# Two-block attention and expert kernel on one core: the context's five products in fp16 parts, correlation factors read from PSUM, and a new order of the step

## What is computed

```python
x = x + L0_xattn(layernorm(x), ctx, ctx)   # autocorrelation: keys and values are both ctx
x = x + L0_ffn(layernorm(x))               # base weight 1024x1024 + 8 experts of rank 16, top 2
x = x + L1_xattn(layernorm(x), ctx)        # 8 heads, window of 16, channels are the 128 rows
x = x + L1_ffn(layernorm(x))               # 4 experts of rank 16, top 2
# L0_xattn: corr = ifft(fft(q) * conj(fft(k))); top 9 lags, softmax of them;
#           out = sum_i w_i * v[min(lag_i + pos, 127)]
# L1_xattn: k = Wk ctx + bk, v = Wv ctx + bv, q = Wq x + bq, softmax over 16 neighbours, Wo
```

## Time and profile before

| what | value |
|---|---|
| median of 3 runs | 2022.52 us (2021.28 to 2024.9) |
| the profiled execution | 2025.97 us |
| its span, first to last instruction | 2024.1 us |
| mean granted TensorE clock | 0.969 |
| busy: PE, DVE, ACT, POOL | 92%, 75%, 67%, 54% |
| weight loads (PEld) | 56% |
| DMA | 45 GB/s mean |

### The profile page before, as it was taken

How to read it: one execution, slowest core, us unless ns; L and a number is a source line. 1 busy time by engine, 2 the same in 40 slices (tenths; PEclk the granted TensorE clock), 3 DMA queues, 4 the chain that set the end, 5 groups by cost and what they waited for, 6 DMA issues and landing times. The chain is left out here.

```text
span 2024.1 us, 49212 instructions
## 1 busy us (share of the span) xinstructions
PE 1855.6 (92%) x18912; PEld 1131.0 (56%) x18912; DVE 1519.6 (75%) x4529; ACT 1347.2 (67%) x1958; POOL 1088.4 (54%) x902
## 2 busy tenths in 40 slices
PE   4889999999999999999999999999999999999975
PEld 2355555665555655555565655566555565655543
DVE  6677777778777778777877777777777877877743
ACT  4267776677776677776667777667777666777652
POOL 2565555466555466555556655546655645655541
PEclk8899999999999999999999999999999999999985
DMA  5001110011111011111001111001111110111000
GB/s 217 22 33 53 52 52 31 31 52 41 52 52 36 27 50 41 52 52 52 31 31 43 50 52 52 31 31 49 45 52 52 44 39 31 41 52 42 21 6 17
DMA packets 25165, 91.56 MB, mean 45 GB/s; under 512 B 3184, under 2 KB 3312, under 8 KB 24624
## 3 DMA queue, kind: packets, MB, share of 16 engines
q1 hardware_dynamic: 25136, 91.17, 12.8%
HBM read 74.39 MB, written 16.78 MB: 45 GB/s over the span
## 5 line engine op out<-in xcount | busy, mean ns | idle before, releaser
L548 PE MATMUL pb<-w_base_h,even_words 128*128 128x512 f16 x1024 | 324.8, 379 | 0.4 <-ACT mid_t L851 0.4
L1370 POOL TENSOR_TENSOR p_hl<-sc,p_hl 128x512 f16<-128x512 f32 x128 | 178.1, 1391 | 180.3 <-ACT p_hl L730 180.3
L450 PE MATMUL pa<-ctx_a,tab 128*128 128x512 f32 x384 | 203.4, 655 | 35.6 <-ACT q_spec L730 24.3
L840 ACT ACTIVATE q_diag<-sc,par 32x1024 f32<-32x1024 f32 x192 | 216.1, 1141 | 19.9 <-DVE sc L1100 17.5
L1413 POOL TENSOR_TENSOR sc<-sc,sc_rec 128x512 f32<-128x512 f32 x128 | 134.2, 1048 | 146.8 <-DVE sc_rec L1176 146.8
L548 PE MATMUL pb<-w_base_l,even_words 128*128 128x512 f16 x512 | 193.9, 379 | 0.0
L617 PEld LDWEIGHTS pc<-sc_t,v_diag 128*128 128x128 f16 x6144 | 173.8, 97 | 32.9 <-issue 23.8
L450 PE MATMUL pa<-xn_a,tab 128*128 128x512 f32 x384 | 186.3, 609 | 1.5 <-ACT xn_a L730 1.5
L617 PE MATMUL pc<-sc_t,v_diag 128*128 128x32 f16 x6144 | 173.9, 177 | 6.5 <-ACT rows_c L730 6.5
L594 PE MATMUL pc<-k_h,q_diag 128*128 128x32 f16 x2048 | 169.1, 177 | 0.0
L595 PE MATMUL pc<-k_l,q_diag 128*128 128x32 f16 x2048 | 168.5, 177 | 0.0
(11 more groups left out here) (149 smaller groups left out, 5068.5 us busy)
## 6 DMA issues: line engine op xcount, KB each, us to landing
x_a<-in_x SPq DMA_DIRECT2D x32, 512.0 KB, 3.3
ctx_a<-in_ctx_in SPq DMA_DIRECT2D x32, 512.0 KB, 3.2
x_res<-in_x SPq DMA_DIRECT2D x32, 512.0 KB, 3.9
ctx_b<-in_ctx_in SPq DMA_DIRECT2D x32, 512.0 KB, 4.0
out<-rows_c SPq DMA_DIRECT2D x32, 512.0 KB, 2.9
v_diag<-in_base_w SPq DMA_DIRECT2D x4, 1024.0 KB, 10.1
tab<-in_spectra SPq DMA_DIRECT2D x1, 576.0 KB, 5.2
q_diag<-in_ra SPq DMA_DIRECT2D x1, 544.0 KB, 13.8
```

The source lines that it names most:

```text
L450: last = mm(place[:, n + h, :], lhsT, moving[:, h * HALF:(h + 1) * HALF], start=True, stop=True)
L548: mm(pb[:, h, :], rows[:, cols], weights[:, j, h * HALF:(h + 1) * HALF], start=(j == 0 and m == 0), stop=False)
L840: nc.scalar.activation(q_diag[rows, :, col:col + QB], source, ACT.Copy, scale=par[rows, a:a + 1]).then_inc(qd_out.sem, 1)
L1370: g_.tensor_tensor(part[:, :, :, LO], sc[:, g % 2, :, :], part[:, :, :, HI], ALU.subtract)\
```

## The change

1. **The context's products.** The context is loaded once a batch (`ctx_f`). ACT copies it to fp16 (`ctx_high`), POOL subtracts (`ctx_low`), into one of two slots of `ctx_hl`. The five tables or weights that meet it (`w_ctx_h`, `w_ctx_l`) are split once. `project_ctx` takes three fp16 matmuls for each half where `project` took a float32 one, for `a_context`, both `a_context_long`, `b_keys` and `b_values`.
2. **Experts.** `b_base_end` becomes six fp16 matmuls, `c_delta` four (high and low halves of the activations are stacked over 128 partitions), `c_mid` one fp16 transposition instead of two float32, `b_mid` two fp16 for one float32. `gates` ends with two more DVE instructions that split `mid`, once for each expert layer. `c_result` is done in two halves.
3. **Correlation's factors.** `q_spec` and the copy to it are gone. DVE forms both products, straight from PSUM. `a_values` is three copies (two of 64 partitions, one of 128) instead of four of 64.
4. **Keys and values** are computed in `pa`, in mid-step, between pieces of the base layer.
5. **Order.** The step is cut at another place (it begins with `a_context_long`), spans indices i to i-3, and is written out for two steps at a time, since the slot alternates. On every engine the calls stand in a new order. `a_corr` is halved, with a long product between the halves.
6. **Start.** All fp16 splits of weights on DVE now stand in one place, after the softmax of batch 0; ACT's stand after the exponents of batch 0. The first `a_context` waits for the split of `ctx_w` and of the context.

```diff
+            def project_ctx(n, slot, table):
+                high, low = ctx_hl[:, slot, 0, :], ctx_hl[:, slot, 1, :]
+                for h in range(2):
+                    cols = slice(h * HALF, (h + 1) * HALF)
+                    mm(pa[:, n + h, :], w_ctx_h[:, table, :], high[:, cols], start=True, stop=False)
+                    mm(pa[:, n + h, :], w_ctx_h[:, table, :], low[:, cols], start=False, stop=False)
+                    last = mm(pa[:, n + h, :], w_ctx_l[:, table, :], high[:, cols], start=False, stop=True)
+                return last
...
+            def ctx_high(b, slot):
+                act.wait_ge(ctx_read.sem, ctx_read.after(b))
+                if not early(b):
+                    act.wait_ge(mm_k.sem, mm_k.after(b - 2))
+                    act.wait_ge(mm_v.sem, mm_v.after(b - 2))
+                copy(ctx_hl[:, slot, 0, :], ctx_f[:, :]).then_inc(ctxh_out.sem, 1)
...
             def a_product(b):
-                dve.wait_ge(q_out.sem, q_out.after(b))
+                dve.wait_ge(mm_q.sem, mm_q.after(b))
                 dve.wait_ge(v_out.sem, v_out.after(b, 2))
-                v.tensor_tensor(c1[:, :], q_spec[:, :], v_re[:, :], ALU.mult).then_inc(prod_q.sem, 1)
+                if not first(b):
+                    dve.wait_ge(mm_agg.sem, mm_agg.after(b - 1))
+                v.tensor_tensor(c2, pa_hi, v_im[:, :], ALU.mult).then_inc(prod_q2.sem, 1)
+                dve.wait_ge(v_out.sem, v_out.after(b))
+                v.tensor_tensor(c1[:, :], pa_hi, v_re[:, :], ALU.mult).then_inc(prod_q.sem, 1)
...
+            def ctx_low(b, slot):
+                pool.wait_ge(ctxh_out.sem, ctxh_out.after(b))
+                g_.tensor_tensor(ctx_hl[:, slot, 1, :], ctx_f[:, :], ctx_hl[:, slot, 0, :], ALU.subtract)\
+                    .then_inc(ctxl_out.sem, 1)
...
+            def b_keys(b, slot):
+                if last_a(b):
+                    pe.wait_ge(prod_w.sem, prod_w.after(b))
+                else:
+                    pe.wait_ge(vagg_out.sem, vagg_out.after(b + 1))
+                project_ctx(2, slot, CTX_K).then_inc(mm_k.sem, 1)
```

More of the change, by code:

```diff
@@ L214, in build @@
         gate_rec = [little(1) for n in range(2)]
-        mid = [sb(f"mid{n}", [P, [P, E1 * RANK][n]]) for n in range(2)]
-        mid_t = [sb(f"mid_t{n}", [[P, E1 * RANK][n], P]) for n in range(2)]
+        mid_hl = [sb(f"mid_hl{n}", [P, 2, [P, E1 * RANK][n]], F16) for n in range(2)]
+        mid0_t = sb("mid0_t", [P, 2, P], F16)
+        mid1_t = sb("mid1_t", [P, P], F16)
+        ident_h = sb("ident_h", [P, P], F16)
         bn = [little(2, 6) for n in range(4)]
@@ new lines, in _ @@
+            for i in range(-2, 6):
+                if i == 0:
+                    pe.wait_ge(tab_in.sem, TABLES_IN)
+                if i == 1:
+                    pe.wait_ge(const_in.sem, CONSTS_IN)
+                    pe.wait_ge(const_set.sem, CONSTS_SET)
+                step(i, i % 2, during(i))
+            with pe.Fori(6, BATCH - 2, 2) as i:
+                step(i, 0, always)
+                step(i + 1, 1, always)
+            for i in range(BATCH - 2, BATCH + 4):
+                step(i, i % 2, during(i))
@@ L730, in copy @@
                 return nc.scalar.activation(dst, src, ACT.Copy)
-            def twice(place, part, signal):
-                rows = slice(part * P // 2, (part + 1) * P // 2)
-                for half in range(2):
-                    copy(place[half * P // 2:(half + 1) * P // 2, :], pa_lo[rows, :]).then_inc(signal.sem, 1)
             def a_norm_rows(b):
@@ L805, in b_values @@
                 act.wait_ge(mm_v.sem, mm_v.after(b))
-                nc.scalar.activation(v_halves[:, PAD:PAD + D, HI], pb_all, ACT.Identity,
+                if not first(b):
+                    act.wait_ge(vt_out.sem, vt_out.after(b - 1))
+                nc.scalar.activation(v_halves[:, PAD:PAD + D, HI], pa_hi, ACT.Identity,
                                      bias=bias_att[:, 2:3]).then_inc(vh_out.sem, 1)
@@ new lines, in _ @@
+            act.wait_ge(ctxw_in.sem, 16)
+            copy(w_ctx_h[:, :, :].rearrange("p n c -> p (n c)"), ctx_w_f32).then_inc(ctxw_hi.sem, 1)
+            for i in range(-2, 6):
+                if i == 0:
+                    act.wait_ge(tab_in.sem, TABLES_IN)
+                    act.wait_ge(const_set.sem, CONSTS_SET)
+                if i == 1:
+                    act.wait_ge(const_in.sem, CONSTS_IN)
+                step(i, i % 2, during(i))
+            with act.Fori(6, BATCH - 2, 2) as i:
+                step(i, 0, always)
+                step(i + 1, 1, always)
@@ new lines, in split_weights @@
+                    quarter = min(part, SPLITS - 1)
+                    cols = slice(quarter * KT * D // SPLITS, (quarter + 1) * KT * D // SPLITS)
+                    place, high, whole = [
+                        (flat_l[:, cols], flat_h[:, cols], base_f32[:, cols]),
+                        (w_ra0_l[:, :, :].rearrange("p k n -> p (k n)"),
+                         w_ra0_h[:, :, :].rearrange("p k n -> p (k n)"), ra0_f32),
+                        (w_b0_l[:, :], w_b0_h[:, :], b0_f32),
+                        (w_b1_l0[low, :], w_b1_hh[low, :], b1_f32[low, :])][max(0, part - SPLITS + 1)]
@@ L1381, in b_value_blocks @@
             def b_value_blocks(b, odd):
+                if first(b) and odd == 0:
+                    pool.wait_ge(vdiag_set.sem, 1)
                 pool.wait_ge(vt_out.sem, vt_out.after(b, odd + 1))
@@ L1393, in b_value_blocks @@
                                  ALU.mult).then_inc(vd_pool.sem, 1)
+                pool.wait_ge(vd_pool.sem, vd_pool.after(b, odd + 1))
             def b_query_blocks(b, a):
+                if first(b) and a == 0:
+                    pool.wait_ge(qdiag_set.sem, 1)
                 if a == 0:
@@ new lines, in step @@
+                if live(0):
+                    pool.wait_ge(sum_w.sem, sum_w.after(i, 1))
+                if live(2):
+                    pool.wait_ge(ln_rs[3].sem, ln_rs[3].after(i - 2))
+                if live(1):
+                    b_query_blocks(i - 1, 0)
+                    b_query_blocks(i - 1, 1)
+                    b_value_blocks(i - 1, 1)
+                if live(0):
+                    root(i, 1)
+                if first(i - 0):
+                    clear_values()
+                if live(1):
+                    c_normalise(i - 1, 0)
@@ L1479 @@
+            pool.wait_ge(power_set.sem, 3)
+            for i in range(-2, 6):
+                if i == 0:
+                    pool.wait_ge(tab_in.sem, TABLES_IN)
+                    pool.wait_ge(const_set.sem, CONSTS_SET)
+                step(i, i % 2, during(i))
+            with pool.Fori(6, BATCH - 2, 2) as i:
+                step(i, 0, always)
+                step(i + 1, 1, always)
+            for i in range(BATCH - 2, BATCH + 4):
+                step(i, i % 2, during(i))
 _OUTS = [((32, 128, 1024), "float32")]
```

869 lines of the change are left out of this document (429 added, 440 removed).

## The result

| what | before | after |
|---|---|---|
| median | 2021.9 us (2018.87 to 2024.9, 4 runs) | 2059.28 us (2052.64 to 2063.73, 4 runs) |
| ratio to before | | 1.0182, 95% interval 1.0149 to 1.0216 |
| profiled execution, span | 2025.97, 2024.1 us | 2052.64, 2050.6 us |
| mean granted clock | 0.969 | 0.936 |
| first residual | 57.48 | 70.38 |

The account below looks back on a forecast made before the run. It took the loop as bound by PE's work until a ring over the engines is longer; 64.5 + 53 + 30 x 56.0 + 17 + 110.3 = 1924.8 us of span, 99 under before, so a median of 1923 us, range 1872 to 1980.

Parts of the forecast that it names:

- to the first residual: Kernel's start up to the first `a_residual`: DVE's and ACT's weight splits add 7 us (0 to 12) to 57.5.
- ring: Dependences over all engines from one end of `b_base_end` to the next, in five items: 56.0 us a step.
- clock: Falls of the granted clock in the loop: ten taken of 0 to 31 possible, 1.70 us each, 17 us.
- end: Stretch behind the last residual: 113.3 less 3 us, from `c_delta` giving back 2 twice and gates taking 0.5 twice.
- What leaves PE: Cheaper fp16 products and one transposition less save PE 3.6 us a step, leaving 53.1 of its own work.
- The rival on the products' price: Six fp16 matmuls on `ctx_hl` take more than 0.215 us each; counted in the longer-ring rival, 24%.
- item 1: From `b_base_end`'s end through DVE's normalisation (0.8 us), squares and root to PE's `rows_to_features`, ending at 10.5 us.
- the idle place: Stretch of the step around `rows_to_features` and the router's wait, where PE does 0.95 us of work in 3.2.
- the event that would refute me: Sign that the prediction is wrong: the clock falls in every step; a third of the steps was expected.
- The rival that ends slower: PE's emptier stretches let the clock fall two or more times a step: 59.4 us a step, about 2035; 3%.
- PE as the bound: The old loop is bound by PE's work, busy 56.68 of 59.59 us a step, with small waits of 2.9.
- the page's doubt: Weight loads busy only 58% of a step suggest PE is not near its bound; the 3.6 us return as waits; 2%.

Follow-up runs that it names:

- the best run: Changed kernel with loops written out, constants' wait moved, seven unread matmuls before stage c's router, POOL's copy in its idle time before the sums: 1903.36 us, ratio 0.9421.

## Why the prediction was wrong, point by point

The span came out 125.8 us over the 1924.8 of the sum:

| term | forecast | measured | over |
|---|---|---|---|
| to the first residual | 64.5 | 70.4 | 5.9 |
| first step | 53 | 57.4 | 4.4 |
| 30 steps, ring alone, with fillers | 30 x 56.0 | 30 x 57.04 | 31 |
| clock | 17 | 67 | 50 |
| jump, with the falls that it brings | 0 | 44 | 44 |
| end | 110.3 | 100.7 | -9.6 |

The three middle rows come from the runs: 57.04 is the step of the run with loops written out and fillers; written out without fillers it is 59.27 (30 x 2.23 = 67), and in after 60.74 (30 x 1.47 = 44).

- **What leaves PE: right.** Distances of 0.215, and 53.1 us of own work where 53.1 was forecast. The rival on the products' price is out.
- **DVE: right in the work, not in its surroundings.** 51.4 busy against 49.3: the normalisation's 1.46 and 1.4 of a softmax whose parts take 467 ns on average instead of 293 are in it. With the copy moved it is 49.9, and the softmax's 1.4 is still in that.
- **The ring, item 1, is the first step that failed:** "Normalising (0.8)". The 0.81 was a duration with no POOL instruction beside it, and the new order puts POOL's copy directly behind the root. I had the order of POOL and did not lay it beside DVE's. With the copy in POOL's gap the step is 55.93, against 56.0. The length comes out, and partly by luck: the path that I followed has a wait of 0.9 for `k_l`, which is not there, and it does not have the softmax's 1.4. Of the Trainium skill's rule (SBUF — State Buffer, SBUF: two separate sides) I had used the exclusion for the start only; 2.27 beside 1.89, begun 0.17 earlier, agrees with it in the loop too, and so do the softmax's parts of 0.78 and 1.37.
- **The clock is the second.** "I take ten, 17 us": it fell in 29 of the 30 steps. I had named the idle place and the event that would refute me, and still took a number from the old kernel's frequency, 6 in 31. The rival that ends slower named the right mechanism, with 3% far too small a chance: it asked for two falls a step, and there were 1.6 (160 us of half clock at 3.4 each), but beside them stood the jump, which the sum does not have at all. That rival's own sum is off: without the ten falls the forecast is 1906, and at 1.70 each a loss begins at 2.3 falls a step, not at 2.1, and with two falls at a ring over 56.5, not 56.2.
- **The jump is the third, a term left out.** "Written out for two steps at a time" stands in my own list of the change and was costed at nothing without a sentence. Nothing in the trace of before shows what such a jump costs, and I did not bound it from either side.
- **Start:** DVE's splits were seen, the constants' wait was not; with it moved the first residual is at 65.25, against 64.5. **First step:** the 53 stands in the sum without a working; it is 2.4 under before. PE is busy only 41.15 of 57.42 there, so it is not the bound, and less work for it cannot give that. **End:** 12.6 shorter instead of 3. No run took it apart; it is 98 to 105 us in all kernels of the new order, 113 and 114 in the old.
- **PE as the bound: half right.** By the rule of the Trainium skill (Trainium Kernel Development and Optimization, Performance Expectations) the share of weight loads, 55%, tells that PE is far from its bound. In the best run PE is busy 54.6 of 55.9 us and weight loads 33.9, 61%, and what it waits is 1.1 us beside the filled place, so the starts and waits told more than that share. But in the change as it is made, the ring, the clock and the jump set the step, and what PE saved came back as waits and as half clock; for that kernel the page's doubt was right.

## What to carry to other kernels

Price every order against both lists at once: a duration is that of an instruction with its neighbours on the other engine, and the copy that costs nothing at one place costs 1.1 us a step at the next. Waits of PE that come together in a step are a reason to count on a lower clock in every step as one of the outcomes, whatever the old kernel's clock did, and then to move what PE waits for, or to fill the wait. And when a loop's body grows, count its instructions: the jump back was free for one step, and for two it cost 2.6 us each time in the new kernel with its clock up, and further falls without.

## What the runs showed that I had not expected

- A jump back stalls PE for 1.6 to 2.2 us and DVE for 1.7 to 2.9 as soon as the body has two steps, with nothing in the trace that ends the wait. Written out, 48 us less; two steps in the kernel before, 34 us more.
- Seven unread matmuls a step (1.5 us of PE) took 77 us off the changed kernel where they stood in a wait, and added 42 where they did not.
- The clock fell in 26 steps in a row with no wait of PE over 0.74 us in all but the first of them (0.65 and 0.74, 1.8 us apart), in one execution of a kernel of which two others kept a mean clock of 0.97. With waits of 1.2, 1.1, 0.8 and 0.7 it mostly did not fall.
- One move had three prices: the copy moved late gave 46 us by itself and nothing beside the fillers; moved on into POOL's gap, with the fillers and no jump, it gave 36.
- Two parts of the softmax on DVE take 0.78 and 1.37 us instead of 0.29 beside POOL's instructions, 1.4 us of DVE a step in every kernel of the new order. No run took this apart.
